# Unread transposes on TensorE in the head of a graph layer, and one statistics block moved behind on VectorE

## What is computed

```python
xn = _layernorm(x, axis=-1)
x = x + _L0_gnn_ref(xn, edge_index, weight, attn_l, attn_r) + _L0_mix_ref(xn[None], Wq, Wk, Wv, Wm, W1, W2, ...)[0]
x = x + _L0_ffn_ref(_layernorm(x, axis=-1)[None], ...)[0]

# in _L0_gnn_ref: only the first n rows of alpha and of the edges are read
xt = jnp.matmul(x, weight).reshape(-1, heads, out_ch)
alpha = softmax(leaky_relu(alpha_l + alpha_r, 0.01), axis=1)
tmp = jnp.einsum('nh,nhd->nd', alpha[:n], xt[col[:n]])

# in _L0_mix_ref
K = jax.nn.elu(k) + 1.0
KV = jnp.einsum('nshd,nshv->nhdv', K, v)
```

## Time and profile before

| | |
|---|---|
| median of 3 runs | 1328.67 us (1327.01 to 1332.3) |
| the profiled execution | 1328.16 us, of which the span of its instructions is 1326.4 us |
| TensorE busy | 1294.6 us, 98% of the span |
| VectorE busy | 1077.4 us, 81% |
| ScalarE busy | 731.6 us, 55% |
| GpSimd busy | 666.7 us, 50% |
| mean granted clock of TensorE | 0.997 of full |

### The profile page before, as it was taken

The page is one execution under the profiler, slowest core; times in us unless marked ns, Lnnn a source line. Parts: engine busy times, 40 slices in busy tenths (PEclk is TensorE's granted clock), DMA queues, the critical chain, the costliest instruction groups (busy, mean ns, idle before and its releaser), DMA issues.

```text
span 1326.4 us, 26270 instructions
## 1 busy us (share of the span) xinstructions
PE 1294.6 (98%) x8812; PEld 1121.4 (85%) x8812; DVE 1077.4 (81%) x2641; ACT 731.6 (55%) x1332; POOL 666.7 (50%) x771
## 2 busy tenths in 40 slices
PE   6999999898999999999999999999999999999998
PEld 6999999776888888888888888888888888888886
DVE  6888777978888888888888888888878888888875
ACT  4555555334645655555645655555645655555654
POOL 5777777746444453444444453444544453444421
PEclk9999999999999999999999999999999999999999
DMA  6787767522122221222121220222121220212000
GB/s 208 241 287 246 254 222 235 153 60 74 40 66 57 80 77 27 72 64 80 39 64 56 80 80 24 74 62 80 41 63 56 80 80 24 76 60 71 25 17 24
DMA packets 65460, 123.24 MB, mean 93 GB/s; under 512 B 31725, under 2 KB 36176, under 8 KB 65422
## 3 DMA queue, kind: packets, MB, share of 16 engines
q1 hardware_dynamic: 57422, 109.25, 25.5%
q0 software_dynamic: 8000, 13.53, 4.6%
HBM read 70.41 MB, written 52.32 MB: 93 GB/s over the span
## 4 chain that ended last, share of the span: by engine, by line
PE 88%; DVE 4%; issue 3%; ACT 2%; POOL 1%; POOLq 1%; DVEq 1%; ACTq 0%
PE psum L272 26%; PE psum L273 25%; PE psum L274 25%; PE psum L484 5%; PE psum L676 3%; PE psum L729 1%; PE psum L667 1%; PE psum L566 1%; PE psum L739 1%; PE psum L559 1%; POOLq L1780 1%; DVE s_lo L1516 0%; POOL ag L1842 0%; POOL xg L1840 0%; POOLq L1836 0%
## 5 line engine op out<-in xcount | busy, mean ns | idle before, releaser
L1846 POOL TENSOR_TENSOR h_lo<-relu,h_hi 128x1024 fp32r<-128x1024 f32 (+1 forms) x50 | 118.4, 2369 | 142.1 <-ACT h_hi L998 142.1
L272 PE MATMUL psum<-w_hi,h_hi 128*128 128x256 f32 x588 | 165.7, 282 | 4.9 <-ACT e L1009 3.1
L273 PE MATMUL psum<-w_lo,h_hi 128*128 128x256 f32 x588 | 165.0, 281 | 0.0
L274 PE MATMUL psum<-w_hi,h_lo 128*128 128x256 f32 x588 | 164.9, 281 | 0.0
L1846 POOL TENSOR_TENSOR s_lo<-relu,s_hi 128x512 fp32r<-128x512 f32 x23 | 29.6, 1289 | 206.0 <-ACT s_hi L1099 206.0
L272 PE MATMUL psum<-z_hi,w_hi 128*128 128x512 f32 (+1 forms) x300 | 121.6, 405 | 2.0 <-DVE z_lo L1616 1.1
L272 PE MATMUL psum<-xT_hi,w_hi 128*128 128x512 f32 (+1 forms) x300 | 118.9, 396 | 0.2 <-DVE relu L1556 0.2
L1840 POOL DMA_INDIRECT xg<-table_xt,idx x100 | 100.5, 1005 | 34.9 <-issue 33.2
L272 PEld LDWEIGHTS psum<-w_hi,h_hi 128*128 128x128 f32 x588 | 111.5, 190 | 7.1 <-ACT e L1009 3.3
L997 ACT ACTIVATE relu<-psum,h_bias 128x512 f32<-128x512 f32 (+1 forms) x100 | 67.8, 678 | 88.9 <-PE psum L274 88.8
L273 PE MATMUL psum<-z_lo,w_hi 128*128 128x512 f32 (+1 forms) x300 | 116.6, 389 | 0.0
(11 more groups left out here) (275 smaller groups left out, 4255.9 us busy)
## 6 DMA issues: line engine op xcount, KB each, us to landing
xb<-in_x SPq DMA_DIRECT2D x47, 448.0 KB, 3.9
xT_hi_table<-x1T_hi SPq DMA_DIRECT2D x25, 512.0 KB, 2.8
xT_lo_table<-x1T_lo SPq DMA_DIRECT2D x25, 512.0 KB, 3.6
xT_hi<-xT_hi_table SPq DMA_DIRECT2D x25, 512.0 KB, 3.8
xT_lo<-xT_lo_table SPq DMA_DIRECT2D x25, 512.0 KB, 4.8
table_xt<-xts SPq DMA_DIRECT2D x24, 455.0 KB, 3.0
out<-xmid SPq DMA_DIRECT2D x24, 448.0 KB, 2.9
xb<-in_x SPq DMA_DIRECT2D x47, 64.0 KB, 4.1
```

The source lines that it names most:

```text
L272: pe.matmul(out, wh, xh, start=first, stop=False)
L273: pe.matmul(out, wh, xl, start=False, stop=False)
L274: return pe.matmul(out, wl, xh, start=False, stop=last)
L1846: ptt(out, src, hi, ALU.subtract).then_inc(S[done], 1)
```

## The change

Two things are changed. On TensorE a helper `keep_clock(n, bank)` issues n transposes of the identity into bank 6 of PSUM, which nothing reads. 38 of them stand ahead of the first transposes, 8 behind each half of the first group's transposes, and 8 behind the transposes of group 1, ahead of the wait for the table weights. On VectorE the statistics of group 2, which stood second in the first turn, stand last in it. The other turns are as before.

```diff
+            def keep_clock(n, bank, at=0):
+
+                for _ in range(n):
+                    pe.transpose(psum[:, bank, at:at + P], ident[:], ident[:])
...
             pe.wait_ge(S["ident"], 1)
+            keep_clock(38, 6)
             for half, done in enumerate(("x1t_first", "x1t")):
                 for j in range(2):
                     pe.wait_ge(S["xn1"], 2 * half + j + 1)
...
                 last.then_inc(S[done], 1)
+                if half == 0:
+                    keep_clock(8, 6)
+            keep_clock(8, 6)
             pe.wait_ge(S["wk_split"], 1)
             pe.wait_ge(S["x1T_first"], 1)
             first_k(0)
             pe.wait_ge(S["x1T"], 1)
             first_k(1).then_inc(S["k_mm"], 1)
             p1_transpose(1, 1)
+            keep_clock(8, 6)
             pe.wait_ge(S["w_split1"], 1)
...
-            def phase1(v, par, more=2):
+            def phase1(v, par, more=2, stats_last=False):
...
-                if more >= 2:
+                if more >= 2 and not stats_last:
                     p1_stats(v + 2, par)
...
                 dve.tensor_copy(k_hi[par][:, 0:t, :], k).then_inc(S["k_hi"], 1)
+                if more >= 2 and stats_last:
+                    p1_stats(v + 2, par)
...
-            phase1(0, 0)
+            phase1(0, 0, stats_last=True)
             phase1(1, 1)
```

## The result

The changed kernel's median over 22 runs is 1332.43 us (1328.28 to 1335.99), that of the kernel before over its 22 runs beside it 1329.78 us (1325.91 to 1333.29). The ratio is 1.0022, with a 95% interval of 1.0013 to 1.0031: slower by 2.9 us (1.7 to 4.1 us; the ratio's share of 1329.78 us), and under the 0.5% that the forecast took as its bound. The profiled execution took 1331.49 us, 1329.8 us of it span.

What follows compares the result with a forecast made beforehand. TensorE, busy 98% of the span, was taken to bound the kernel, so head delays move the end: 2.1 us late tiles plus 2.2 us clock fall, 4.3 us on 1328.16 us, forecast 1332.5 us; 8-in-10 range 1327.3 to 1334.6 us.

Steps and rivals of the forecast that it cites:

- the 0.5% that the forecast took as its bound: Whole kernel: a measurement can tell about 0.5%, 6.6 us, from no change; same 0.91, slower 0.06, faster 0.03.
- TensorE enters the turns late by what its group 2 is late: Head: group 2's late statistics delay turn 1's tables from 26.29 to 28.35 us; 2.1 us later, bounds 1.7 and 2.5.
- The transposes cost nothing and lift the clock: Before 9.18 us on TensorE: the 38 cost 0 to 0.1 us and the clock is high at the first product.
- The eights: Sets of 8 unread transposes in TensorE's first turn: cost 0, the first two with up to 0.1 us in either direction.
- 24 products, first tables, products of group 1: TensorE's first turn: products with Wk end at 14.80 us, tables start at 16.55 us, group 1's products at 20.78 us.
- The clock falls in the new hole, 2.2 us: TensorE's wait for group 2 from 23.72 us: clock falls between 26 and 28.5 us, costing 2.2 us (1.5 to 2.9).
- the third rival: Head: transposes don't lift the clock; turn 1's tables 5.2 us late, 1333.4 us, up to 1336 us; chance 0.12.
- The faster rival: Head: group 2's tiles are there in time, tables start 1.8 us earlier than before; 1326.4 us; chance 0.12.
- Its reserve: Head, the faster rival's support: ScalarE had 1.1 us of slack, and interference between operations may have been read too high.
- The rival with nothing to tell: Near 322.6 us: shifted, the old hole may pass without its 2.6 us clock fall; 1329.9 us or less; chance 0.06.
- with the clock held: Rival, head: the clock doesn't fall in the new hole, only the 2.1 us stand; 1330.4 us; chance 0.2.

Runs made afterwards that it cites:

- the hole filled: Changed kernel plus 24 unread transposes between group 1's products with Wk and the wait for group 2's first tile; 1.0024 and, again, 1.0015 of the kernel before.
- the second comparison: The changed kernel itself, unaltered, timed again beside the kernel before on another chip; 1329.80 us against 1326.13 us, ratio 1.0027.
- changed kernel, third time: The changed kernel itself, unaltered, timed once more beside the kernel before on a third chip; 1329.74 us against 1328.40 us, ratio 1.0008.
- the statistics alone: Changed kernel without any unread transposes, group 2's statistics still last in the first turn; 1332.52 us against 1326.91 us before, ratio 1.0044.
- the cast on ScalarE: Changed kernel with group 2's statistics back in second place and group 0's cast (xr_hi) moved from VectorE to ScalarE; 1327.75 us, 1.0006 of before.
- transposes only: Changed kernel with its unread transposes but group 2's statistics back in their old second place; 1327.95 us against 1326.91 us before, ratio 1.0007.
- the first four variants: Transposes only, the statistics alone, the hole filled (first time) and the cast on ScalarE, on one chip; the kernel before beside them took 1326.91 us.

## Why the prediction was right, and where it wasn't

- **TensorE enters the turns late by what its group 2 is late**: right. Statistics ended at 22.89 us (I had 23.51), GpSimd's chain took 2.40 us (2.4), ScalarE 2.08 us (2.07), tables at 27.81 us (28.35). The term measures 1.5 us, not 2.1 us (1.5 to 1.9 us over the three profiles of the changed kernel). What was too high is the end of the statistics, by 0.6 us: the first operation on `kf` was taken with its old 1.07 us and took 0.69 us, and it started at 16.96 us and not at 17.22 us.
- **The transposes cost nothing and lift the clock**: right, in every kernel with them (it rose between 4.5 and 7.5 us). The eights cost at most 0.1 us; the first product was at 12.08 us instead of 11.86 us, because VectorE made `wk_hi` at 10.18 us and not at 9.72 us, behind a later load of group 1.
- **24 products, first tables, products of group 1**: 14.91, 16.57 and 20.60 us, forecast as 14.80, 16.55 and 20.78 us.
- **The clock falls in the new hole, 2.2 us**: this step fell as a constant. It falls in three of five profiles, and costs 1.35 to 1.5 us where it does, low for 3.4 us and not for the 6.8 us of the earlier trace rows. Over executions that is some 0.8 us (an estimate: 3/5 of 1.4 us) and not 2.2 us. Filling the hole gave nothing that the timing can tell.
- **The number**: that 1332.5 us was forecast and 1332.43 us measured is luck. The difference was forecast as 4.3 us and is 2.65 us between the medians of the 22 runs, 1.65 us too much; it was added to the profiled execution's 1328.16 us, which lies 1.62 us under the median of the kernel before, 1329.78 us. The two errors cancel. The three comparisons of the changed kernel (1.0022, 1.0027, 1.0008) hold about 1 us beyond the 1.5 us of the head, which the falls in the hole could nearly make up, but the comparison with the hole filled does not show it.
- That last part stays open. In the second comparison the changed kernel's mean clock is under that of before (0.9956 against 0.9967), in the third over it (0.9969 against 0.9962), and the ratio goes the same way (1.0027, 1.0008). So falls of the clock at changing places (in the hole, and between the phases, where every unfilled profile with a late head has one) are the likeliest cause, together with the long form of VectorE's subtraction, but no variant singled them out.
- **The rule in the Trainium skill** ("TensorE: Matmul & The Clock Gate", "Part 4: PE-mode transpose"), that the high clock doesn't set in for transposes, is contradicted here: the clock rose at 4.7 us with transposes alone on the engine. The measurement decides, and the third rival did not happen in any of the nine kernels with these transposes.
- **The faster rival** would have needed VectorE to be through with group 2 by 20.1 us; it was at 22.89 us. Its reserve, that I might have read the interference too high, was real (0.4 us) and too small.
- **The rival with nothing to tell** had its condition met in the profile: there was no fall near 325 us. The 1329.9 us that it gives did not follow, as this execution had lost 5.3 us more between the phases.
- One sum was off in its last digit: with the clock held, 1328.16 + 2.1 is 1330.3 us and not 1330.4 us.

## What to carry to other kernels

Work moved off one result of an engine is moved onto another: here two results of VectorE, one for TensorE's next products and one for those behind them, were in balance, and the one sent behind took three engines' latencies with it. A faster start of the engine that waits anyway only lengthens its next wait, and the clock can fall behind it. Unread transposes lift the clock, and with them in the waits it stayed up more often. They belong into waits whose length is known and that no reordering can remove, and their gain has to be looked for in the granted clock over many runs, as it is smaller than the spread of the times. And a forecast of one or two microseconds should say what the same kernel's profiles differ by among themselves, here up to 6 us from the order of two starts.

## What the runs showed of the hardware

- Transposes alone raise TensorE's clock: 0.19 us each until 4.7 us, 0.10 us each from there. The clock rose at 4.5 to 7.5 us in the nine kernels with the 38 transposes and at 14.6 to 18.0 us in the five without.
- VectorE's tensor_scalar of 128x1024 f32 that begins while GpSimd's subtraction runs ends a fixed time behind it, here in all eight profiles with that order. `xr_lo` ends at 19.52, 19.42 and 19.47 us in the kernel before, with the statistics alone and with the cast on ScalarE; the tensor_scalar of 128x1024 starts at 19.00, 17.16 and 18.54 us, takes 1.07, 2.82 and 1.48 us, and so ends 0.55 to 0.56 us behind it each time. Started 0.16 us ahead of `xr_lo`, in the changed kernel, it took its 0.69 us, and `xr_lo` 2.77 us instead of 2.38 us.
- Near 315 us a start 0.33 us ahead does not protect VectorE: its subtraction takes 6.16 us and ends 1.1 us behind the second of GpSimd's two. Started 1 us behind the first of them it takes 2.83 us, and they take 6.03 us instead of 4.74 us.
- The issue of GpSimd's indirect load takes 0.95 us, and 1.94 us where it starts 0.10 us behind a tensor_tensor of VectorE (128x1024 f32, 1.23 us).
- The clock can fall behind a wait of 1.84 us (transposes only) and hold through one of 1.65 us at the same place (cast on ScalarE) and through one of 2.80 us elsewhere (changed kernel, third time).
- Over the 32 runs of the kernel before beside the first four variants, the 12 with a mean granted clock of 0.999 have a median of 1325.76 us and the 15 with 0.996 or less 1328.62 us.
